# Silu from ScalarE's table two tiles at a time, and part of a state-space scan in PSUM, in a fused scan and expert kernel

## The chip, the cores and the metric

The kernel runs on one core of one Trainium2 chip. A core has TensorE (matrix products into PSUM), VectorE, ScalarE, GpSimd (POOL) and SyncE (SP, which issues transfers), each with its own instruction stream, tied by semaphores. The metric is device time in microseconds, the median of three runs. Lower is better.

## The reference

The input x is 2 x 2048 x 256, in fp32. After a layer norm two blocks run on it, and both are added to x.

```python
# block 1: tokens sorted by cluster, then for 256 channels and 16 states
dA = exp(d_t[..., None] * A)
h = dA * h + (d_t * u_t)[..., None] * b_t[:, None, :]
y = einsum('bdn,bn->bd', h, c_t)          # + D * u, and back to the old order
# block 2: 8 experts, top 2 of each token
h = silu(xt @ w1[e]) * (xt @ w3[e]);  y = h @ w2[e]
```

## The kernel before

A preparation makes the layer norm, the clusters, the gates, the sorted rows and, per chunk of 512 tokens, delta, delta * u, B and C, which go to DRAM (`dd_d`, `bc_d`). Then comes the loop. It has 64 **units** u (8 chunks c of 512 tokens, G = 8 groups g of 32 channels), and beside unit u stands expert tile j = u (128 tokens of one expert); 71 tiles in all, so the last seven form a tail. A partition of a unit is one of 32 channels and one of four sets of states; NH = 4 states lie beside one another along the row.

In unit u:

- SP loads the rows of delta and delta * u (`load_dd`), `late<-dd_d`, two buffers. ScalarE copies delta * u into the PSUM tile `pd` (`put_du`, L631) once VectorE's second product of the unit before has read the old one, and makes exp(delta * A) for the unit to come in one of four buffers of `ring` (`exps`, L620).
- VectorE runs `silu(j)` (L1009, L1012), then twice `half_unit`: a product delta * u * B of two states, 1024 wide, into PSUM `pb` (L968), and two scans of 512 from `ring` and `pb` into `ring` (L977). `keep_states` (L984) takes the four last columns.
- GpSimd multiplies the states by C in place (`multiply`, L473), two products of 1024, and then issues the gather of tile rows (L453) and the scatter-add of a finished tile (L460). In groups 3 and 6 it scatters two finished row blocks of the chunk before (L467) between its products, which are then 512 and 1536 wide.
- TensorE folds the products over states (`fold_states`, L1151, two units later), turns y (L1159), and for the expert tile runs `up` (four products with w1 into `fa`, four with w3 into `fb`, L1218), turns h (L1204) and the next x (L1188), the skip term (L1224) and `down` (w2, L1229). PSUM `pt` is shared by the turned h and the turned x; `py` by the down product, the folded sum and the turned y.
- ScalarE also runs `tanh(j)` (L688) on `fa`, and copies the turned h (L694), y rows (L641), the folded sum (L648), turned x (L654) and the weighted tile (L702) out of PSUM.

Each engine's order is written out by hand, one loop pass per tile; TensorE's is up(j), turn h(j-1), turn y(j-3), fold(j-2), turn x(j+1), skip and down(j-1). SP has one queue: weights of w3 and w2 for experts 0, 1 and 2 are loaded in the preparation and for 3 to 7 (ten loads of 512 KB) at unit 2, between the rows of unit 2 and those of unit 3.

## Time and profile before

| | us |
|---|---|
| median of three runs | 797.51 (797.41 to 798.80) |
| the profiled execution | 798.66 |
| its span | 796.9 |
| VectorE busy in the span | 681.3 (85%) |
| TensorE busy (modelled ends) | 650.7 (82%) |
| GpSimd busy | 596.8 (75%) |
| ScalarE busy | 420.1 (53%) |

The span is the time from the first to the last instruction that the profiler saw; the execution has 1.8 us around it. The shares are means over preparation, loop and tail. In rows of a timeline the first number is the start in us, the second the duration in us; xN merges N instructions; a bracket at the end gives the engine's idle time just before and what ended it. PE is TensorE, DVE VectorE, ACT ScalarE, POOL GpSimd. PEclk is the granted clock of TensorE as a share of 2.4 GHz.

### The profile page before, as it was taken

Reading aid. Unit: us, or ns where it says so; the run is one execution under the profiler, and the core shown is the slowest. Engines: PE = TensorE matmul, PEld = TensorE weight load, DVE = VectorE, ACT = ScalarE, POOL = GpSimd, SP = SyncE. Lnnn points to the kernel's source line nnn. Section 1 sums busy time; section 2 is a strip of 40 time slices with the busy share of each in tenths; the row PEclk is TensorE's granted clock in tenths of the full one; section 3 lists DMA queues with packets and bytes.
Section 4 is the critical chain, followed back from the end, with each engine's and each line's share of the span. In section 5 each row is a group of like instructions: output and inputs, shape, how many; then the busy total and the mean of one; then the engine's idle time right before and its main releaser. Section 6 shows DMA issues by size and latency. Waiting matters only on the chain.

```text
span 796.9 us, 13845 instructions
## 1 busy us (share of the span) xinstructions
PE 650.7 (82%) x4602; PEld 424.9 (53%) x4602; DVE 681.3 (85%) x883; ACT 420.1 (53%) x910; POOL 596.8 (75%) x371
## 2 busy tenths in 40 slices
PE   2633977777988898887989898899879898988992
PEld 1413855344655555655656555566556565555662
DVE  5858858897999999999899999989998999999120
ACT  1323657836666555655555655556555566554220
POOL 3727820166878889998989998888989899989642
PEclk9965989898999999999999999989989999999997
DMA  7982689996556744764475457537644754342331
GB/s 211 370 292 86 193 259 381 319 323 172 108 106 131 160 90 97 163 141 94 107 160 123 102 132 151 114 79 164 131 93 107 168 117 101 80 93 41 47 44 23
DMA packets 66275, 116.97 MB, mean 147 GB/s; under 512 B 12104, under 2 KB 46496, under 8 KB 64160
## 3 DMA queue, kind: packets, MB, share of 16 engines
q1 hardware_dynamic: 44048, 88.78, 38.5%
q0 software_dynamic: 19824, 27.16, 19.8%
q8 instruction: 40, 0.66, 0.3%
q10 hardware_dynamic: 2336, 0.15, 0.2%
q14 instruction: 27, 0.22, 0.1%
HBM read 80.78 MB, written 35.27 MB: 146 GB/s over the span
## 4 chain that ended last, share of the span: by engine, by line
DVE 38%; POOL 23%; PE 12%; issue 11%; DMA 11%; SPq 3%; ACT 2%; DVEq 0%; POOLq 0%; ACTq 0%
DVE ring L977 20%; POOL ring L473 11%; DVE pb L968 10%; POOL out_dram L460 4%; POOL out_dram L467 4%; DMA out_dram<-pool,tab 3%; PE py L1229 3%; DMA dd_d<-pool 3%; DVE pool L1009 2%; POOL pool L453 2%; DMA ring<-in_L_attn_x_dram 2%; PE fa L1218 2%; PE fb L1218 2%; PE py L1166 1%; POOL w2x L436 1%
## 5 line engine op out<-in xcount | busy, mean ns | idle before, releaser
L473 POOL TENSOR_TENSOR ring<-ring,bc 128x1024 f32<-128x1024 f32 (+1 forms) x127 | 305.9, 2426 | 34.2 <-DVE state L984 31.7
L977 DVE TENSOR_TENSOR_SCAN ring<-ring,state,pb 128x512 f32<-128x512 f32 x256 | 313.8, 1267 | 4.5
L620 ACT ACTIVATE ring<-late,aneg 128x512 f32<-128x512 f32 x256 | 164.6, 728 | 10.9 <-DMA late<-dd_d 10.9
L968 DVE TENSOR_TENSOR pb<-fb,bc 128x1024 f32<-128x1024 f32 x128 | 157.3, 1229 | 2.2
L1229 PE MATMUL py<-w2x,pool 128*128 x568 | 141.0, 393 | 0.0
L460 POOL DMA_INDIRECT out_dram<-pool,tab x71 | 113.7, 1602 | 34.0 <-DMA out_dram<-pool,tab 14.4
L1218 PE MATMUL fa<-w,pool 128*128 x284 | 136.3, 603 | 2.2 <-ACT pool L654 2.2
L1218 PE MATMUL fb<-w,pool 128*128 x284 | 133.5, 592 | 0.0
L453 POOL DMA_INDIRECT pool<-xn_d,tab x71 | 71.3, 1004 | 66.3 <-DVE ids L932 31.4
L1229 PEld LDWEIGHTS py<-w2x,pool 128*128 128x128 f32 x568 | 107.4, 200 | 12.9
L1151 PE MATMUL py<-ring,fold 128*32 128x128 f32 x2048 | 71.7, 282 | 26.9 <-POOL ring L473 26.9
L1218 PEld LDWEIGHTS fb<-w,pool 128*128 128x128 f32 x284 | 53.6, 191 | 65.8 <-issue 65.8
L688 ACT ACTIVATE pool<-fa 128x512 f32<-128x512 f32 x71 | 42.3, 596 | 83.2 <-PE fa L1218 83.2
L1224 PE MATMUL py<-skip,pool 128*128 128x128 f32 x284 | 51.1, 305 | 35.4 <-ACT y L648 29.9
L1009 DVE SCALAR_TENSOR_TENSOR pool<-pool,fa 128x512 f32<-128x512 f32 x71 | 48.2, 678 | 37.2 <-ACT pool L688 37.1
L1218 PEld LDWEIGHTS fa<-w,pool 128*128 128x128 f32 x284 | 54.8, 194 | 41.6 <-issue 37.9
L1151 PEld LDWEIGHTS py<-ring,fold 128*32 128x32 f32 x2048 | 53.7, 112 | 39.3 <-POOL ring L473 30.5
L1224 PEld LDWEIGHTS py<-skip,pool 128*128 128x128 f32 x284 | 39.6, 202 | 50.0 <-ACT late L641 42.8
L694 ACT COPY pool<-pt 128x512 f32<-128x512 f32 x71 | 41.5, 584 | 45.9 <-PE pt L1204 45.8
L467 POOL DMA_INDIRECT out_dram<-late,ids x32 | 50.5, 1578 | 15.5 <-issue 8.7
L641 ACT COPY late<-py 128x128 f32<-128x128 f32 x64 | 17.0, 265 | 83.4 <-PE py L1151 82.2
L1012 DVE SCALAR_TENSOR_TENSOR pool<-pool,fb 128x512 f32<-128x512 f32 x71 | 48.7, 686 | 9.0 <-PE fb L1218 6.9
(214 smaller groups left out, 732.8 us busy)
## 6 DMA issues: line engine op xcount, KB each, us to landing
late<-dd_d SPq DMA_DIRECT2D x256, 128.0 KB
bc<-bc_d SPq DMA_DIRECT2D x64, 256.0 KB
w<-in_L_ffn_w_dram SPq DMA_DIRECT2D x16, 512.0 KB, 7.7
ring<-in_L_attn_x_dram SPq DMA_DIRECT2D x8, 512.0 KB, 4.3
out_dram<-ring SPq DMA_DIRECT2D x8, 512.0 KB, 6.7
xn_d<-w2x SPq DMA_DIRECT2D x8, 512.0 KB, 8.0
dd_d<-pool SPq DMA_DIRECT2D x8, 512.0 KB, 7.1
w2x<-in_L_ffn_w_dram SPq DMA_DIRECT2D x8, 512.0 KB
```

The costliest lines, as they stand in the source:

```text
L453: po.indirect_dma_start(xr[j % XR], None, xn_d[:, :], bass.IndirectOffsetOnAxis(ap=tab.bitcast(U32)[:, j, 0:1], axis=0)).then_inc(xr_in[j ...
L460: po.indirect_dma_start(out[:, :], bass.IndirectOffsetOnAxis(ap=tab.bitcast(U32)[:, j, 0:1], axis=0), ye[j % YE], None, compute_op=ALU.add ...
L467: po.indirect_dma_start(out[:, :], bass.IndirectOffsetOnAxis(ap=ids[:, TPC * c + n:TPC * c + n + 1], axis=0), ya[c % 2][:, n, :], None, co ...
L473: return po.tensor_tensor(r, r, bc[:, u // G % 2, 1, states, :].rearrange("p n c -> p (n c)"), ALU.mult)
L620: ins = ac.activation(ring[:, u % RING, n, :], dd[:, u % 2, 0, :], ACT.Exp, scale=aneg[:, NH * g + n:NH * g + n + 1])
L968: ve.tensor_tensor(pb[:, :].rearrange("p (n c) -> p n c", n=2), pd[:, :].rearrange("p (o c) -> p o c", o=1).to_broadcast([P, 2, CH]), bc[: ...
L977: ve.tensor_tensor_scan(r, r, pb[:, CH * m:CH * m + CH], state[:, NH * g + n:NH * g + n + 1], ALU.mult, ALU.add).then_inc(S["scan_done"], 1)
L1009: ve.scalar_tensor_tensor(t, t, 1.0, fa[j % 2][:, :], ALU.add, ALU.mult).then_inc(S["s1_done"], 1)
L1151: ins = pe.matmul(pz[DG * q:DG * q + DG, 256:384], fold[:, :], ring[:, u % RING, n, P * q:P * q + P], start=(n == 0), stop=(n == NH - 1), ...
L1218: ins = pe.matmul(dst[:, :], xt[j % XT][:, P * k:P * k + P], w[:, bass.ds(e * (KC * H) + H * k, H)], start=(k == 0), stop=(k == KC - 1))
L1224: pe.matmul(py[:, P * k:P * k + P], xt[j % XT][:, P * k:P * k + P], skip[:, P * k:P * k + P], start=(k == 0), stop=False)
L1229: ins = pe.matmul(py[:, 0:D], ht[:, P * k:P * k + P], w2[:, bass.ds(e * (HC * D) + D * k, D)], start=False, stop=(k == HC - 1))
```

## The change

- `tanh(j)` becomes `gate(j)`, which takes silu from ScalarE's table "silu_and_others"; the exps need "exp_and_others". From tile 3 on ScalarE computes the gates of tiles j and j + 1 together in the passes of odd j, so the tables are changed twice in two tiles. TensorE therefore runs the w1 products of both tiles in the odd pass, on both sides of turn h, and turned x is made two tiles ahead.
- VectorE's silu is one product of the gate and `fb`. `silu(0)` moves behind unit 0.
- In groups 3, 4, 6 and 7 (not in unit 63) the fourth state is scanned into `pb`; VectorE multiplies it by C into `ring`, and copies its last column apart. GpSimd multiplies three states there.
- SP: expert 2's weights move from the preparation to unit 2; three experts are loaded before unit 3's rows and three behind them. SP itself waits until an expert's two loads have landed and counts that in `w_landed`, on which TensorE waits; behind unit 3's rows it waits for experts 2 to 7 before it goes on to the rows of unit 4.

```diff
 UNITS = NCH * G
-REST = UNITS + 1
+REST = UNITS + 2
+SINGLE = 3
+SHARED = (3, 4, 6, 7)
...
 HOT = 3
-EARLY = 3
+EARLY = 2
...
             eng.sem_inc(S["passed"], 1)
...
+        def shared(u):
...
+            return u % G in SHARED and u != UNITS - 1
...
+        def shares_by(u):
...
+            return sum(shared(v) for v in range(u + 1))
...
                 sp.dma_start(w2[:, e * HC * D:(e + 1) * HC * D].rearrange("p (k d) -> p k d", k=HC),
-                             w2_in[e].rearrange("(k p) d -> p k d", p=P)).then_inc(S["w2_in"], 16)
+                             w2_in[e].rearrange("(k p) d -> p k d", p=P)).then_inc(S[f"w_in{e}"], 16)
...
+            def count_landed(e):
...
+                sp.wait_ge(S[f"w_in{e}"], 32)
+                sp.sem_inc(S["w_landed"], 1)
...
                     load_down(0)
-                if c in (3, 4):
-                    if c == 3:
-                        sp.wait_ge(S["tab_ready"], 1)
-                    load_up(c - 2, w3, w3_in)
-                    load_down(c - 2)
+                if c == 3:
+                    sp.wait_ge(S["tab_ready"], 1)
+                    count_landed(0)
+                    load_up(1, w3, w3_in)
+                    load_down(1)
...
                     load_dd(1)
+                    count_landed(1)
...
                     load_dd(u)
-                if u == 2:
+                for e in {2: range(EARLY, 5), 3: range(5, E)}.get(u, ()):
+                    load_up(e, w3, w3_in)
+                    load_down(e)
+                if u == 3:
                     for e in range(EARLY, E):
-                        load_up(e, w3, w3_in)
-                        load_down(e)
+                        count_landed(e)
...
                         sp.wait_ge(S["hc_done"], G * c)
+                        sp.wait_ge(S["hd_done"], len(SHARED) * c)
...
                 if u < UNITS - 1:
-                    done = multiply(u, slice(split, NH))
+                    done = multiply(u, slice(split, NH - 1 if shared(u) else NH))
...
-            def tanh(j):
+            def gate(j):
                 ac.wait_ge(S["a_done"], j + 1)
-                ac.activation(sg[:, j % 2, :], fa[j % 2][:, :], ACT.Tanh, scale=0.5).then_inc(S["tanh_done"], 1)
+                if j >= 2:
+                    ac.wait_ge(S["htr_done"], j - 1)
+                ac.activation(sg[:, j % 2, :], fa[j % 2][:, :], ACT.Silu).then_inc(S["gate_done"], 1)
...
             exps(0)
-            tanh(0)
+            ac.preload_act_table_set("silu_and_others")
+            gate(0)
             evac_xt(1)
+            ac.preload_act_table_set("exp_and_others")
...
                 u = j
-                tanh(j)
+                first = j < SINGLE or j % 2
+                if first:
+                    ac.preload_act_table_set("silu_and_others")
+                    if j > 1:
+                        gate(j)
...
                     put_du(u)
+                if j == 1:
+                    gate(j)
                 evac_ht(j - 1)
+                if first:
+                    if j >= SINGLE:
+                        gate(j + 1)
+                    if u + 1 < UNITS:
+                        ac.preload_act_table_set("exp_and_others")
...
                     take_sum(u - 2)
-                if j + 1 < FT:
-                    evac_xt(j + 1)
+                ahead = j + 1 if j < SINGLE else j + 2
+                if ahead < FT:
+                    evac_xt(ahead)
...
                 evac_y(j - 1)
+                if j == SINGLE - 1:
+                    evac_xt(j + 2)
...
                     ve.wait_ge(S["scan_done"], 4 * u + 2 * half2)
+                if u and half2 == 0 and shared(u - 1):
+                    ve.wait_ge(S["hd_done"], shares_by(u - 1))
+                    ve.wait_ge(S["low_kept"], shares_by(u - 1))
...
                     n = 2 * half2 + m
-                    r = ring[:, u % RING, n, :]
-                    ve.tensor_tensor_scan(r, r, pb[:, CH * m:CH * m + CH], state[:, NH * g + n:NH * g + n + 1],
+                    r, b = ring[:, u % RING, n, :], pb[:, CH * m:CH * m + CH]
+                    ve.tensor_tensor_scan(b if n == NH - 1 and shared(u) else r, r, b, state[:, NH * g + n:NH * g + n + 1],
...
                 ve.wait_ge(S["scan_done"], 4 * u + 4)
-                ve.tensor_reduce(state[:, NH * g:NH * g + NH], ring[:, u % RING, :, CH - 1:CH], AX, ALU.max).then_inc(S["h_ready"], 1)
+                if not shared(u):
+                    ve.tensor_reduce(state[:, NH * g:NH * g + NH], ring[:, u % RING, :, CH - 1:CH], AX, ALU.max).then_inc(S["h_ready"], 1)
+                    return
...
+                top = pb[:, CH:2 * CH]
+                ve.tensor_reduce(state[:, NH * g:NH * g + NH - 1], ring[:, u % RING, 0:NH - 1, CH - 1:CH], AX, ALU.max).then_inc(S["h_ready"], 1)
+                ve.tensor_tensor(ring[:, u % RING, NH - 1, :], top, bc[:, u // G % 2, 1, NH - 1, :], ALU.mult).then_inc(S["hd_done"], 1)
+                ve.tensor_copy(state[:, NH * g + NH - 1:NH * g + NH], top[:, CH - 1:CH]).then_inc(S["low_kept"], 1)
...
-                ve.wait_ge(S["tanh_done"], j + 1)
+                ve.wait_ge(S["gate_done"], j + 1)
+                ve.wait_ge(S["b_done"], j + 1)
                 t = sg[:, j % 2, :]
-                ve.scalar_tensor_tensor(t, t, 1.0, fa[j % 2][:, :], ALU.add, ALU.mult).then_inc(S["s1_done"], 1)
-                ve.wait_ge(S["s1_done"], j + 1)
-                ve.wait_ge(S["b_done"], j + 1)
-                ve.scalar_tensor_tensor(t, t, 0.5, fb[0][:, :], ALU.mult, ALU.mult).then_inc(S["silu_done"], 1)
+                ve.tensor_tensor(t, t, fb[0][:, :], ALU.mult).then_inc(S["silu_done"], 1)
...
                 half_unit(u, 0)
+                half_unit(u, 1)
+                keep_states(u)
...
                     silu(u)
-                half_unit(u, 1)
-                keep_states(u)
...
                     ve.wait_ge(S["h_ready"], u + 1)
+                    ve.wait_ge(S["low_kept"], shares_by(u))
...
                     pe.wait_ge(S["hc_last"], 1)
+                if shared(u):
+                    pe.wait_ge(S["hd_done"], shares_by(u))
...
-            def expert_landed(name, j, e):
+            def expert_landed(j, e):
                 if j <= G:
-                    pe.wait_ge(S[name], e * 16 + 16)
+                    pe.wait_ge(S["w_landed"], e + 1)
...
                 pe.wait_ge(S["silu_done"], j + 1)
+                ahead = j + 2 if j + 1 < SINGLE else j + 3
+                pe.wait_ge(S["xt_done"], min(ahead, FT))
...
-            def up(j, e):
+            def up(j, e, w, dst, done):
+                for k in range(KC):
+                    ins = pe.matmul(dst[:, :], xt[j % XT][:, P * k:P * k + P],
+                                    w[:, bass.ds(e * (KC * H) + H * k, H)], start=(k == 0), stop=(k == KC - 1))
+                ins.then_inc(done, 1)
...
+            def up_gate(j, e):
                 pe.wait_ge(S["xt_done"], j + 1)
-                for w, dst, done in ((w1, fa[j % 2], S["a_done"]), (w3, fb[0], S["b_done"])):
-                    if w is w3:
-                        expert_landed("w3_in", j, e)
-                        if j:
-                            pe.wait_ge(S["silu_done"], j)
-                        if j >= REST:
-                            turn_h(j - 1)
-                    for k in range(KC):
-                        ins = pe.matmul(dst[:, :], xt[j % XT][:, P * k:P * k + P],
-                                        w[:, bass.ds(e * (KC * H) + H * k, H)], start=(k == 0), stop=(k == KC - 1))
-                    ins.then_inc(done, 1)
+                if j >= 2:
+                    pe.wait_ge(S["gate_done"], j - 1)
+                up(j, e, w1, fa[j % 2], S["a_done"])
...
+            def up_value(j, e):
...
+                expert_landed(j, e)
+                if j:
+                    pe.wait_ge(S["silu_done"], j)
+                up(j, e, w3, fb[0], S["b_done"])
...
                               stop=False)
-                expert_landed("w2_in", j, e)
...
             pe.wait_ge(S["pr_ut"], KC * (NCH - 1))
-            up(0, e_down)
+            up_gate(0, e_down)
...
             turn_x(1)
+            up_value(0, e_down)
...
                 u = j
+                e_next = expert_of(j + 1) if j + 1 < FT else None
                 if j == G + 1:
-                    pe.wait_ge(S["w3_in"], 16 * E)
-                    pe.wait_ge(S["w2_in"], 16 * E)
-                up(j, e_up)
-                e_next = expert_of(j + 1) if j + 1 < FT else None
-                if j < REST:
+                    pe.wait_ge(S["w_landed"], E)
+                if j < SINGLE:
+                    up_gate(j, e_up)
+                    up_value(j, e_up)
+                    turn_h(j - 1)
+                elif j % 2:
+                    up_gate(j, e_up)
+                    turn_h(j - 1)
+                    up_gate(j + 1, e_next)
+                    up_value(j, e_up)
+                else:
+                    up_value(j, e_up)
...
                 pe.wait_ge(S["ht_done"], j)
-                if j + 1 < FT:
-                    turn_x(j + 1)
+                ahead = j + 1 if j < SINGLE else j + 2
+                if ahead < FT:
+                    turn_x(ahead)
...
                 down(j - 1, e_down)
+                if j == SINGLE - 1:
+                    pe.wait_ge(S["xt_done"], j + 2)
+                    turn_x(j + 2)
```

VectorE, from the end of one unit to the next unit's first product. Before:

```order
L977 SCALAR_TENSOR_TENSOR ring<-ring,state,pb 128x512
L984 TENSOR_REDUCE state<-ring 128x4 [waits scan_done]
L1009 SCALAR_TENSOR_TENSOR pool<-pool,fa 128x512 [waits tanh_done]
L1012 SCALAR_TENSOR_TENSOR pool<-pool,fb 128x512 [waits b_done,s1_done]
L968 TENSOR_TENSOR pb<-fb,bc 128x1024 [waits scan_done,du_put]
```

After, behind a shared unit (group 4):

```order
L1017 SCALAR_TENSOR_TENSOR pb<-ring,state,pb 128x512
L1029 TENSOR_REDUCE state<-ring 128x3 [waits scan_done]
L1030 TENSOR_TENSOR ring<-pb,bc 128x512
L1031 COPY state<-pb 128x1
L1057 TENSOR_TENSOR pool<-pool,fb 128x512 [waits b_done,gate_done]
L1008 TENSOR_TENSOR pb<-fb,bc 128x1024 [waits hd_done,low_kept,scan_done,du_put]
```

One of the two silu steps is gone, and two instructions and one scan's target are new; the next unit's first product has two more waits.

TensorE, from the w1 products of an odd tile on (`fa1`), repeated rows left out. Before:

```order
L1218 ISA [waits xt_done]
L1218 MATMUL fa1<-w1,pool 128x512
...
L1218 REGISTER_ALU [waits silu_done]
L1218 MATMUL fb0<-w3,pool 128x512
...
L1204 MATMUL pt<-ident,pool 128x128 [waits silu_done]
...
L1159 MATMUL py<-ident,y1 128x128 [waits ya_done,y1_done,ye_done]
L1151 MATMUL py<-ring,fold 32x128 [waits y1_done,hc_done]
...
L1188 MATMUL pt<-ident,pool 128x128 [waits xr_in0,ht_done]
...
L1224 MATMUL py<-skip,pool 128x128 [waits y1_done,ya_done]
```

After, an odd tile and the start of the even one:

```order
L1259 ISA [waits gate_done,xt_done]
L1259 MATMUL fa1<-w1,pool 128x512
...
L1254 MATMUL pt<-ident,pool 128x128 [waits xt_done,silu_done]
...
L1259 ISA [waits gate_done,xt_done]
L1259 MATMUL fa0<-w1,pool 128x512
...
L1259 REGISTER_ALU [waits silu_done]
L1259 MATMUL fb0<-w3,pool 128x512
...
L1207 MATMUL py<-ident,y1 128x128 [waits ya_done,y1_done,ye_done]
L1199 MATMUL py<-ring,fold 32x128 [waits y1_done,hc_done]
...
L1236 MATMUL pt<-ident,pool 128x128 [waits xr_in1,ht_done]
...
L1259 REGISTER_ALU [waits silu_done]
L1259 MATMUL fb0<-w3,pool 128x512
```

The even tile's w1 products (`fa0`) moved ahead of the odd tile's w3 products (`fb0`).

ScalarE, from the weighted tile (L702, now L723) through the copies of one tile. Before:

```order
L702 ACTIVATE pool<-py,tab 128x256 [waits added,w2_done]
L688 ACTIVATE pool<-fa1 128x512 [waits a_done]
L631 COPY fb1<-late 128x512 [waits dbu_done]
L694 COPY pool<-pt 128x512 [waits htr_done]
L641 COPY late<-py 128x4x32 [waits sum_done,ytr_done]
L648 COPY y1<-py 128x128 [waits ytr_done,sum_done]
```

After, an odd tile:

```order
L723 ACTIVATE pool<-py,tab 128x256 [waits added,w2_done]
L737 ACT_TABLE_LOAD
L709 ACTIVATE pool<-fa1 128x512 [waits htr_done,a_done]
L650 COPY fb1<-late 128x512 [waits dbu_done]
L715 COPY pool<-pt 128x512 [waits htr_done]
L709 ACTIVATE pool<-fa0 128x512 [waits htr_done,a_done]
L749 ACT_TABLE_LOAD
L660 COPY late<-py 128x4x32 [waits added,sum_done,ytr_done]
L667 COPY y1<-py 128x128 [waits ytr_done,sum_done]
L673 COPY pool<-pt 128x256 [waits xtr_done]
```

Two table loads and a second gate stand in the odd pass; both gates are there, and the even pass has none.

## Rows read from the trace of the kernel before

**Rows 1.** Busy time; columns: stretch, us, PE, PEld, DVE, ACT, POOL, granted clock
```profile
200.00:735.00 535.00, 474.30 (x3502) 306.60 (x3504) 517.71 (x536) 308.25 (x647) 473.56 (x265) 0.97 0.54 117
```

**Rows 2.** Timeline of VectorE, one unit: start, duration (us)
```profile
507.25 0.16 DVE L984 TENSOR_REDUCE state<-ring 128x4 f32<-128x4 f32 x1
507.32 0.68 DVE L1009 SCALAR_TENSOR_TENSOR pool<-pool,fa 128x512 f32<-128x512 f32 x1
508.04 0.69 DVE L1012 SCALAR_TENSOR_TENSOR pool<-pool,fb 128x512 f32<-128x512 f32 x1
508.64 1.23 DVE L968 TENSOR_TENSOR pb<-fb,bc 128x1024 f32<-128x1024 f32 x1
...
516.14 0.16 DVE L984 TENSOR_REDUCE state<-ring 128x4 f32<-128x4 f32 x1
```

**Rows 3.** Timeline of VectorE, ends of units 0, 4 and 63
```profile
161.93 0.16 DVE L984 TENSOR_REDUCE state<-ring 128x4 f32<-128x4 f32 x1
...
202.42 0.16 DVE L984 TENSOR_REDUCE state<-ring 128x4 f32<-128x4 f32 x1
...
734.50 0.16 DVE L984 TENSOR_REDUCE state<-ring 128x4 f32<-128x4 f32 x1
```

**Rows 4.** Timeline of GpSimd and TensorE, a unit with scatter-adds, and an earlier fold
```profile
417.78 1.08 PE L1151 MATMUL py<-ring,fold 128*32 128x128 f32 x32 [1.71 <-POOL ring L473]
...
507.81 1.28 POOL L473 TENSOR_TENSOR ring<-ring,bc 128x512 f32<-128x512 f32 x1
...
513.26 4.02 POOL L473 TENSOR_TENSOR ring<-ring,bc 128x1536 f32<-128x1536 f32 x1
...
517.34 1.08 PE L1151 MATMUL py<-ring,fold 128*32 128x128 f32 x32 [3.00 <-POOL ring L473]
```

**Rows 5.** Busy time and granted clock (column after POOL) in two stretches
```profile
420.00:422.00 2.00, 2.00 (x7) 1.82 (x8) 1.96 (x3) 2.00 (x5) 1.98 (x2) 0.52 0.94 188
520.00:522.00 2.00, 2.00 (x8) 1.73 (x8) 1.97 (x3) 2.00 (x4) 1.97 (x2) 0.50 0.60 120
```

**Rows 6.** Timeline, TensorE's tile while it chases VectorE
```profile
526.72 1.88 PE L1218 MATMUL fb<-w,pool 128*128 x4
...
528.71 0.69 DVE L1012 SCALAR_TENSOR_TENSOR pool<-pool,fb 128x512 f32<-128x512 f32 x1 [0.47 <-PE fb L1218]
...
537.18 1.08 PE L1151 MATMUL py<-ring,fold 128*32 128x128 f32 x32
...
538.96 0.68 PE L1224 MATMUL py<-skip,pool 128*128 128x128 f32 x4 [0.33 <-ACT y L648]
...
541.21 1.88 PE L1218 MATMUL fa<-w,pool 128*128 x4
...
545.28 0.97 PE L1151 MATMUL py<-ring,fold 128*32 128x128 f32 x28
```

**Rows 7.** Timeline, TensorE's tile while it is ahead of VectorE
```profile
235.51 0.59 ACT L631 COPY fb<-late 128x512 f32<-128x512 f32 x1 [1.56 <-DVE pb L968]
...
238.08 0.68 PE L1224 MATMUL py<-skip,pool 128*128 128x128 f32 x4 [0.98 <-ACT y L648]
```

**Rows 8.** The page's costliest groups; count, busy us, mean ns, idle before
```profile
L977 DVE TENSOR_TENSOR_SCAN ring<-ring,state,pb 128x512 f32<-128x512 f32 x256 | 313.8, 1267 | 4.5
...
L968 DVE TENSOR_TENSOR pb<-fb,bc 128x1024 f32<-128x1024 f32 x128 | 157.3, 1229 | 2.2
```

**Rows 9.** Timeline of ScalarE, the one table load near the loop
```profile
154.06 1.28 ACT L688 ACT_TABLE_LOAD   x1
155.35 0.60 ACT L688 ACTIVATE pool<-fa 128x512 f32<-128x512 f32 x1
```

**Rows 10.** The chain that ended last: first weight load, unit 3's rows
```profile
156.34 0.43 SPq L283
...
171.20 10.04 DMA late<-dd_d
```

**Rows 11.** Waits between 100 and 165 us; in total, times, longest
```profile
DVE pool L943 <- DMA dd_d<-pool: 2.8, 2, 2.1
```

8 lines of the change are left out of this document (4 added, 4 removed).

## The prediction, made before the changed kernel ran

> **What bounds the kernel now.** I read the busy time by stage first. Up to some 154 us the tokens are prepared; from there 64 scan units run, until 735 us; then comes a tail of expert tiles. The stretch that matters is the loop [rows 1]. In the 535 us from 200 to 735 VectorE is busy 517.7 us (97%), GpSimd 473.6, TensorE 474.3 (modelled), ScalarE only 308.3. So the length of a VectorE unit sets the loop. One unit row by row [rows 2]: from reduce to reduce 516.14 - 507.25 = 8.89 us. In starts: reduce 0.07, the silu's first step 0.72, its second 0.60, then twice a product and its two scans, 7.50 in all (508.64 to 516.14).
>
> Next, where VectorE waits. Units 0 and 4 end at 161.93 and 202.42 [rows 3]: 40.49 for four, 4.9 more than 4 x 8.89, all of it at unit 3, which waits for its rows. Unit 63 ends at 734.50, which is 532.1 us for 59 units; 59 x 8.89 is 524.7, so 7.4 us are lost in the loop. They lie nearly all at units 25, 41 and 49. For unit 41 [rows 4, 5]: unit 38 ends at 507.25, GpSimd puts two scatter-adds between its products, whose last starts at 513.26 and ends at 517.28; TensorE has waited 3.00 us at the fold; then it runs at half clock for some 6 us (granted 0.50, 1.2 GHz), and VectorE is released late, at 528.71.
>
> How far off is TensorE as a bound? In a stretch where it chases [rows 6] its tile takes 537.18 to 545.28 = 8.10 us: fold to skip 1.78, skip and down 2.25 (538.96 to 541.21), w1 and w3 products 1.72 each, turning h and y 0.64 (4.07 from 541.21 to 545.28). Where it is ahead, it is tied to VectorE through ScalarE [rows 7]: the copy of du to PSUM starts as soon as the unit's second product has read the old one, at 235.51, 2.5 before the unit's end, and the skip starts 2.57 later.
>
> **The change part by part.**
>
> VectorE, silu. L1009 (71 times) goes, L1012 becomes a plain product of the same 128x512. Removed: 0.72 a unit. The new form has no row. The two nearest agree: the old second step, of the same operands, takes 0.69 (0.60 in starts); the 1024-wide product takes 1229 ns [rows 8], 1.04 ns an element above a fixed 160 if the 512-wide step is put beside it. Ends: 0.05 less and 0.05 more. I take no difference: a plain unit is 8.17.
>
> VectorE, shared units (3, 4, 6, 7 of each eight; not the last): the product with C, 512 wide out of PSUM, is added: 0.60 in starts; the one-column copy 0.07, as the reduce (158 ns, nearly all covered by its successor). 0.67 a unit. A scan that writes PSUM has no row. The nearest is L968 [rows 8], which already writes PSUM and shows no price for it; so 0. The other end is a scan that takes twice its 1.27 us (rival (d)); a gain is not expected, since a scan of 512 takes 1267 ns where a product of 512 takes 686: its steps, not its operands, set the length.
>
> Units 5 to 63: minus 59 x 0.72 = 42.5, plus 30 shared predecessors x 0.67 = 20.1: **22.4 less**.
>
> GpSimd: in shared units 512 elements less. A product of 512 takes 1.28 [rows 4], one of 1024 half of a pair's 4.69: 1.1 us less. It is relieved by 4.3 per eight units where VectorE is by 8 x 0.72 - 4 x 0.67 = 3.1, so it comes no nearer to being the bound.
>
> ScalarE: two table loads per two tiles in the loop. A load is 1.28 us and the next ACTIVATE starts at once [rows 9]. Silu for tanh: 0.60 for 0.60. ScalarE goes from 308/535 = 58% to about 58% x 8.89/8.51 + 2.57/17.0 = 75%. What hides them: the silu load lies after the old tile's y, beside the w1 products (skip + 2.24, a_done at + 4.1; y, load end at + 4.2), 0.1 late at most and for a value needed at + 8.1. The exp load lies beside the w3 products and the fold: ScalarE is through at + 9.25, and the fold at + 8.05 can be evacuated 1.20 later, at + 9.25. That is exact cover, with nothing over.
>
> TensorE: the same products in other order. Odd tile: w1 of j, turn h, w1 of j+1, w3 of j. After an even tile's skip, w3 of the odd tile starts at 2.25 + 1.72 + 0.44 + 1.71 = 6.12 and is seen done 1.99 later (526.72 to 528.71 [rows 6]), 8.11 in all. Tied to VectorE (skip 2.57 behind the du copy, which stands 2.6 before the next silu), it is done 10.68 after the du copy; VectorE wants it at 2.60 + 8.17 = 10.77 in the tightest case (third of eight). Slack 0.09; now, with 2.57 + 2.25 + 3.44 = 8.3 for the w3 products, it is nearly 4. A pair of tiles takes 16.2 at best against VectorE's mean pair of 17.0: TensorE keeps up, barely. So stalls stay. Where unit 6's scatters delay the fold: now it starts 517.34 - 507.41 = 9.9 after the unit's end; less 1.1 of product and about 0.8, since the add before the scatters comes sooner, it is about 8; the odd tile behind it (9th) is done at 8.0 + 1.8 + 8.1 = 17.9, wanted at 2 x 8.84 + 0.07 = 17.75. A few tenths, unless the clock halves, 3.3 us each. TensorE's idle time before that fold I work out as about 1.6 us (now 3.0); before other folds 1.71 us also was followed by half clock [rows 4, 5], so I count two halvings of six. Stalls: 2 x 3.3 + 1.4 for the rest = **8.0, against 7.4: 0.6 more**.
>
> SP and start. Unit 3's rows now stand behind 10 weight loads of 512 KB, the first issued at 156.34, and come in at 181.24 [rows 10]; after, behind 6. Ten loads and the rows in 24.9 us are 2.3 a load; alone on the queue a load would take 1.4 (0.52 MB at the page's best slice, 381 GB/s). So they land 5.6 to 9 sooner, before 176. Against it: expert 2's 1 MB moves from the preparation into this burst, SP then waits for all weights before it issues unit 4's rows (now issued before 175), and ScalarE's du copy of unit 4 is queued behind those exps. Also unit 1's w3 products now wait for silu(0), which moved behind unit 0. In order: preparation 1.3 sooner (VectorE waits 2.8 there for stores that stand behind expert 2's weights [rows 11]; bounds 0 and 2.8); unit 0 1.2 shorter, since silu(0) leaves it; unit 1 starts 2.1 after VectorE is free; unit 2 plain; unit 3 waits 1.0 for gate(3) behind a table load; unit 4 waits 1.8 for its du copy. The ends become 159.4, 170.3, 178.5, 187.7, 198.3 in place of 202.42: **4.1 less**, bounds 1 and 7.
>
> The tail, 62.4 us from unit 63's end to the span's end, is one of TensorE's tiles and their landing; its products are the same. 0, give or take 1.
>
> **Sum** against the profiled execution: 798.66 - 22.4 + 0.6 - 4.1 = 772.8; the median of the runs is 1.15 lower: 771.6.
>
> **Rivals.**
>
> (a) TensorE late: its idle time before unit 6's folds is not shorter and the clock halves in all seven. 5 more x 3.3 = 16.5: 788. For it: 3 of 6 do now, and slack is gone. Against: the faster product.
>
> (b) A table load costs more than its row, by as much again. The silu load has 4 us of room, the exp load none: the pair is 16.2 + 1.28 = 17.48 against 17.02, 0.46 x 30 pairs = 13.8: 785.4. Against it: 155.35 follows 154.06 by 1.29. Of this the Trainium skill, "ScalarE: Activation LUTs", What ACT_TABLE_LOAD costs, says that a load of 1283 ns has a drain of about 1380 ns behind it, and its Table sets section advises against changing sets in turns; this trace agrees with the 1283 and shows no drain. By the page's drain the sum would be an estimated 788.
>
> (c) Rows not sooner: SP's wait for all weights brings unit 4's rows so late that the start gains nothing: 775.7.
>
> (d) **Slower**: a scan that reads and writes one PSUM tile runs at half pace, 2.54 for 1.27: 31 x 1.27 = 39.4: 811. It is slower than before from 0.84 us a scan on. Nothing in the trace scans into PSUM.
>
> (e) (b) with four of (a)'s five extra halvings: 785.4 + 13.2 = 798.6, no change.
>
> **How the numbers follow.** Forecast 0.67, (a) 0.09, (b) 0.07, (c) 0.07, (d) 0.07, (e) 0.03. Likeliest: 771.6. The low end is no halving and all of the preparation's gain: 771.6 - 6.6 - 1.5 = 763.5; the high end takes in (a), (b) and (c), 788.5; (d) and (e) are left out, 0.10, and some tails. A measurement of this kernel can tell about 0.2% from no change. Faster 0.90, same 0.03, slower 0.07.
>
> **What would show it.** VectorE's unit of 8.17 and 8.84 in the trace after, the new product about 0.69, the scan into PSUM 1.27; unit 4's end near 198; table loads 1.28 each, 60-odd; VectorE's waits in the loop near 8 us, at the ninth units and on the w3 products. Wrong if the scan or the product out of PSUM is longer, if TensorE's pair is above 17.0, or if waits for gate or du appear in each pair.

## The result, and the profile after

| | before | after |
|---|---|---|
| median of the runs | 797.46 us | 788.42 us (783.5 to 795.57) |
| ratio to before | 1 | 0.986, 95% interval 0.981 to 0.990 |
| profiled execution's span | 796.9 | 793.9 |
| end of unit 0 / 4 / 63 | 161.93 / 202.42 / 734.50 | 163.43 / 204.18 / 732.47 |
| from unit 63's end to the span's end | 62.4 | 61.4 |

Forecast was 771.6 with a range of 763.5 to 788.5. The changed kernel is 1.0 to 1.9% faster, not 3.2%. Its runs spread over 12 us, and the profiled one is its longest; two more profiles of the same kernel stand below and are used beside it. They belong to other measurements on other chips, with medians of 784.26 us (0.982, 0.978 to 0.987) and 786.78 us (0.976, 0.970 to 0.982). Medians here are over all runs of a kernel, but the ratios leave out its slow runs, those over 1.5% above its fastest: one of four above, and three of the six behind 786.78, whose median is 782.31 without them.

VectorE's units first, as in [rows 2]: the timeline of one shared unit (start, duration, us), from the previous unit's end to this one's.

```profile
509.19 0.16 DVE L1029 TENSOR_REDUCE state<-ring 128x3 f32<-128x3 f32 x1
509.27 0.68 DVE L1030 TENSOR_TENSOR ring<-pb,bc 128x512 f32<-128x512 f32 x1
509.87 0.15 DVE L1031 COPY state<-pb 128x1 f32<-128x1 f32 x1
509.93 0.68 DVE L1057 TENSOR_TENSOR pool<-pool,fb 128x512 f32<-128x512 f32 x1
510.53 1.22 DVE L1008 TENSOR_TENSOR pb<-fb,bc 128x1024 f32<-128x1024 f32 x1
...
515.54 1.28 DVE L1017 TENSOR_TENSOR_SCAN ring<-ring,state,pb 128x512 f32<-128x512 f32 x1
516.74 1.26 DVE L1017 TENSOR_TENSOR_SCAN pb<-ring,state,pb 128x512 f32<-128x512 f32 x1
518.03 0.16 DVE L1029 TENSOR_REDUCE state<-ring 128x3 f32<-128x3 f32 x1
```

From reduce to reduce 8.84 us, the forecast's number. The scan into PSUM takes 1.26, as the one into SBUF; the product out of PSUM 0.68 (0.60 in starts), the copy 0.06 in starts, the silu's one step 0.60. A unit behind an unshared one takes 8.18.

The unit ends that answer to [rows 3], and the loop's busy times that answer to [rows 1] (stretch, us, PE, PEld, DVE, ACT, POOL, granted clock):

```profile
163.43 0.16 DVE L1025 TENSOR_REDUCE state<-ring 128x4 f32<-128x4 f32 x1
...
204.18 0.16 DVE L1029 TENSOR_REDUCE state<-ring 128x3 f32<-128x3 f32 x1
...
217.10 0.16 DVE L1025 TENSOR_REDUCE state<-ring 128x4 f32<-128x4 f32 x1
...
732.47 0.16 DVE L1025 TENSOR_REDUCE state<-ring 128x4 f32<-128x4 f32 x1
```

```profile
200.00:735.00 535.00, 481.64 (x3546) 309.96 (x3545) 501.39 (x540) 385.26 (x714) 443.37 (x267) 0.97 0.55 119
```

VectorE is now idle for 34 of 535 us instead of 17. Units 5 to 63 would take 502.1 (59 x 8.17 + 30 x 0.67); they took 732.47 - 204.18 = 528.3, so 26.2 us are lost where I had counted 8.0: 19.2 at six units, 4.1 at unit 5, the rest in small pieces. Behind unit 5 nearly all of it is one wait, for the w3 products (VectorE's waits between 213 and 700 us: in total, times, longest):

```profile
DVE pool L1057 <- PE fb L1259: 20.5, 9, 3.8
```

The 19.2 stand at units 17, 25, 33, 41, 49 and 57, which the forecast calls the ninth units: always at the odd tile behind the fold of a unit 6. Around unit 41, as [rows 4], GpSimd, TensorE and VectorE:

```profile
511.44 1.60 POOL L486 DMA_INDIRECT out_dram<-late,ids  x1 [0.73 <-DMA out_dram<-pool,tab]
...
513.34 1.56 POOL L486 DMA_INDIRECT out_dram<-late,ids  x1 [0.30 <-issue]
...
514.33 2.94 POOL L492 TENSOR_TENSOR ring<-ring,bc 128x1024 f32<-128x1024 f32 x1
...
517.33 1.08 PE L1199 MATMUL py<-ring,fold 128*32 128x128 f32 x32 [2.46 <-POOL ring L492]
...
521.01 3.10 PE L1283 MATMUL py<-w2x,pool 128*128 x8
...
529.81 0.69 DVE L1057 TENSOR_TENSOR pool<-pool,fb 128x512 f32<-128x512 f32 x1 [2.78 <-PE fb L1259]
```

The unit before ended at 509.19. The fold starts 8.1 us later, where I had put it; but TensorE has idled for 2.46, not 1.6, and the down products behind it take 3.10 instead of the 1.89 of an undisturbed tile. The 7 us behind each of the six folds (the last three columns are the granted clock, the DMA share and GB/s):

```profile
302.00:309.00 7.00, 6.81 (x47) 5.32 (x48) 6.86 (x10) 3.28 (x8) 6.01 (x4) 0.54 0.43 95
375.20:382.20 7.00, 6.63 (x50) 4.99 (x51) 6.89 (x7) 4.37 (x9) 5.56 (x4) 0.76 0.38 78
447.20:454.20 7.00, 6.82 (x50) 4.89 (x51) 6.72 (x10) 4.66 (x9) 5.14 (x4) 0.76 0.43 96
517.30:524.30 7.00, 5.72 (x47) 4.62 (x48) 6.90 (x9) 3.30 (x8) 5.93 (x4) 0.76 0.42 105
588.60:595.60 7.00, 6.91 (x47) 5.43 (x48) 6.86 (x10) 3.26 (x8) 6.17 (x4) 0.53 0.44 96
660.90:667.90 7.00, 5.75 (x48) 4.57 (x49) 6.89 (x8) 3.44 (x8) 5.98 (x4) 0.76 0.40 80
```

TensorE drops to its lower level (0.5 is 1.2 GHz) behind all six, for part or all of the stretch. Before, it did so behind three of six. The same 7 us in the kernel before, in front of units 33 (no fall) and 41 (fall):

```profile
445.10:452.10 7.00, 6.07 (x52) 4.23 (x53) 6.86 (x7) 3.97 (x9) 6.37 (x4) 1.00 0.36 77
517.30:524.30 7.00, 6.04 (x47) 4.92 (x48) 6.90 (x7) 3.25 (x7) 6.52 (x4) 0.63 0.29 52
```

The start: SyncE, ScalarE and VectorE around unit 4's rows.

```profile
176.20 0.47 SPq L350 DMA_DIRECT2D w2x<-in_L_ffn_w_dram  x1
...
178.86 2.56 ACT L639 ACTIVATE ring<-late,aneg 128x512 f32<-128x512 f32 x4 [0.75 <-DMA late<-dd_d]
...
186.35 0.69 DVE L1057 TENSOR_TENSOR pool<-pool,fb 128x512 f32<-128x512 f32 x1 [2.42 <-PE fb L1259]
...
188.22 1.72 SPq L339 DMA_DIRECT2D late<-dd_d  x4
...
193.23 2.56 ACT L639 ACTIVATE ring<-late,aneg 128x512 f32<-128x512 f32 x4 [5.04 <-DMA late<-dd_d]
```

Unit 3's rows do come sooner: their exponentials start at 178.86, not 181.27 [rows 10], and SyncE issues the last of the weights at 176.20. But then it waits for them, unit 4's rows are issued at 188.22, and its exponentials wait 5.04 us. VectorE waits 2.42 at unit 3, and unit 5 ends at 217.10, 12.9 behind unit 4. Whether SyncE's wait is what brings these rows late is tried below.

The difference from the forecast's span (772.8 less the 1.76 around it, 771.0) adds up: unit 4 ends 5.9 late, the loop loses 18.2 more, the tail is 1.0 shorter, 23.1 in all; 793.9 - 771.0 = 22.9.

### The profile page after: what moved, and what is told of

The parts are those of the page before. It is cut to its first block, busy times and chain, and to the rows that moved or that the text cites. A ratio compares the mean times of both kernels' runs of the same rounds, so it can differ in the third digit from the quotient of the medians.

```text
span 793.9 us, 14137 instructions
## 1 busy us (share of the span) xinstructions
PE 660.6 (83%) x4602; PEld 428.7 (54%) x4602; DVE 654.3 (82%) x874; ACT 506.9 (64%) x979; POOL 562.8 (71%) x371
## 4 chain that ended last, share of the span: by engine, by line
DVE 32%; POOL 21%; PE 17%; DMA 13%; issue 11%; SPq 3%; ACT 2%; DVEq 0%; ACTq 0%; POOLq 0%
DVE ring L1017 16%; DVE pb L1008 9%; POOL ring L492 7%; DMA out_dram<-pool,tab 6%; POOL xs_d L448 5%; POOL out_dram L486 4%; PE fa L1259 4%; PE py L1283 3%; DMA out_dram<-late,ids 2%; PE py L1199 2%; PE fb L1259 2%; POOL out_dram L479 2%; DVE pb L1017 2%; DMA w2x<-in_L_ffn_w_dram 1%; PE py L1279 1%
## 5 line engine op out<-in xcount | busy, mean ns | idle before, releaser
L492 POOL TENSOR_TENSOR ring<-ring,bc 128x1024 f32<-128x1024 f32 (+1 forms) x127 | 272.3, 2162 | 48.4 <-DVE state L1025 34.4
L1017 DVE TENSOR_TENSOR_SCAN ring<-ring,state,pb 128x512 f32<-128x512 f32 x225 | 277.5, 1269 | 4.6
L479 POOL DMA_INDIRECT out_dram<-pool,tab x71 | 112.7, 1587 | 43.7 <-DMA out_dram<-pool,tab 16.5
L1283 PE MATMUL py<-w2x,pool 128*128 x568 | 142.6, 397 | 0.0
L1259 PE MATMUL fb<-w,pool 128*128 x284 | 135.3, 599 | 3.1 <-DVE pool L1057 3.1
L1283 PEld LDWEIGHTS py<-w2x,pool 128*128 128x128 f32 x568 | 109.0, 202 | 13.3
L1057 DVE TENSOR_TENSOR pool<-pool,fb 128x512 f32<-128x512 f32 x71 | 48.5, 683 | 67.3 <-PE fb L1259 67.2
L1259 PEld LDWEIGHTS fb<-w,pool 128*128 128x128 f32 x284 | 54.3, 192 | 56.9 <-issue 55.2
L650 ACT COPY fb<-late 128x512 f32<-128x512 f32 x64 | 37.8, 590 | 59.8 <-DVE pb L1008 59.7
L1259 PEld LDWEIGHTS fa<-w,pool 128*128 128x128 f32 x284 | 51.6, 192 | 39.5 <-issue 37.7
L1279 PEld LDWEIGHTS py<-skip,pool 128*128 128x128 f32 x284 | 40.0, 203 | 49.3 <-ACT late L660 44.1
L1254 PEld LDWEIGHTS pt<-ident,pool 128*128 128x128 f32 x284 | 35.8, 142 | 37.8 <-issue 37.7
L448 POOL DMA_INDIRECT xs_d<-w2x,pos_a x32 | 38.3, 1196 | 23.6 <-DVE pos_a L885 14.1
## 6 DMA issues: line engine op xcount, KB each, us to landing
w2x<-in_L_ffn_w_dram SPq DMA_DIRECT2D x8, 512.0 KB, 10.7
```

The source lines that it names most:

```text
L448: po.indirect_dma_start(dst[:, :], bass.IndirectOffsetOnAxis(ap=index[:, t:t + 1], axis=0), row[:, t, 0:dst.shape[1]], None).then_inc(done ...
L479: po.indirect_dma_start(out[:, :], bass.IndirectOffsetOnAxis(ap=tab.bitcast(U32)[:, j, 0:1], axis=0), ye[j % YE], None, compute_op=ALU.add ...
L492: return po.tensor_tensor(r, r, bc[:, u // G % 2, 1, states, :].rearrange("p n c -> p (n c)"), ALU.mult)
L1017: ve.tensor_tensor_scan(b if n == NH - 1 and shared(u) else r, r, b, state[:, NH * g + n:NH * g + n + 1], ALU.mult, ALU.add).then_inc(S["s ...
L1259: ins = pe.matmul(dst[:, :], xt[j % XT][:, P * k:P * k + P], w[:, bass.ds(e * (KC * H) + H * k, H)], start=(k == 0), stop=(k == KC - 1))
L1279: pe.matmul(py[:, P * k:P * k + P], xt[j % XT][:, P * k:P * k + P], skip[:, P * k:P * k + P], start=(k == 0), stop=False)
```

## The experiments

All times below are medians of 6 or 12 runs of a kernel; the kernel before, beside them, had 797.96 to 800.20. A ratio is to it, with its 95% interval. The changed kernel ran beside the experiments on two of the five chips only; where it didn't, kernels are compared by their ratios.

**The changed kernel twice more.**

> The changed kernel once more, unchanged. Theory N (the number of half-clock episodes differs from run to run): the median stays at 786 to 790 and a second profile has VectorE's units at 8.18 and 8.84 again, but its stalls at the ninth units sum to another number than the 26 us of the first profile, by 3 us or more, and its start of the loop lies 1 to 3 us elsewhere. Theory F (all of the lost time is in the order of the work): the stalls are the same within 1 us.

> The changed kernel, unchanged, as the measure of the other kernels on this chip: by both theories 784 to 790, its stalls at the ninth units 14 to 23 us together, each behind a fold that starts 8.0 to 10.3 us after unit 6's end and at which TensorE had waited over 2.2 us.

Measured 784.26 (0.982, 0.978 to 0.987) and, on another chip, 786.78 us. Stalls at the ninth units: 19.2 us in the first profile, 15.4 and 19.2 in these. The fold behind unit 6 starts 9.1 us after the unit's end in the mean of the 18 cases (8.1 to 10.3), TensorE idle before it for 2.8 (1.8 to 4.0), and the clock falls behind all 18. Unit 4 ends at 200.49 and 201.71, and unit 5 takes 8.9 in both: the 4 us lost there in the first profile come and go. From unit 5 on the loop loses 26.2, 16.3 and 20.0 us in the three, so theory N holds and F falls, though the median of 784.26 is below N's 786. Of the first profile's shortfall some is luck of that run; the stalls at the ninth units are not.

These profiles also show the slack of each place, as the time from the modelled end of a tile's w3 products to the silu product that reads them, less the 0.11 us that is left where VectorE waits. In front of the third unit of eight it is 0.16 us (0.09 forecast), in front of the ninth, where no scatters delay the fold (unit 9), 1.65, and at even tiles from tile 4 on 2.0 to 4.4.

**Clock or lateness.** TensorE kept busy ahead of the late fold.

```diff
+WARM = 24
...
-                pe.transpose(pz[:, 384:512], y1[:, :], ident[:, :]).then_inc(S["ytr_done"], 1)
+                for _ in range(WARM if u % G == G - 3 and u > G else 1):
+                    ins = pe.transpose(pz[:, 384:512], y1[:, :], ident[:, :])
+                ins.then_inc(S["ytr_done"], 1)
```

> Ahead of each fold that waits for GpSimd's two scatters of unit 6, TensorE repeats the transposition of y 24 times instead of once, some 2.5 us of work in an idle stretch of 2.5. Theory B1 (the stalls at every ninth unit are the half clock behind that idle stretch, 3.3 us each): the granted clock stays at full behind these folds, each stall falls from about 3.4 to about 0.8 us, six times, so 14 to 16 us less, 772 to 774. Rival B2 (the stalls are the late fold alone, and the clock only goes with it): 788, no change, or longer by the added work, up to 3 us.

Measured 777.80 us (0.974, 0.971 to 0.978), 6.5 less than the changed kernel on the same chip. The granted clock behind the six folds, first and last:

```profile
295.50:302.50 7.00, 6.65 (x56) 4.61 (x57) 6.89 (x9) 5.75 (x11) 6.18 (x4) 1.00 0.41 87
...
644.70:651.70 7.00, 6.64 (x56) 4.59 (x57) 6.86 (x10) 5.76 (x11) 6.18 (x4) 1.00 0.45 96
```

It is 1.00 in all six, and the stalls at the ninth units fall from 15.4 to 6.7 us. B1 holds for the cause, not for the size: with the clock kept up, 0.3 to 1.7 us stay at each, which is the late fold itself, and two of the folds were now late behind the repeats. By the difference to the profiles above (15.4 and 19.2) the clock costs 1.5 to 2.1 us at each of the six; the lateness costs about 1.1.

The repeats are not the only evidence. In two kernels below, whose folds behind unit 6 are as in the changed kernel, the clock stayed up once each by itself. One is the changed kernel with silu(0) moved back. The fold in front of its unit 33, and the 7 us behind it:

```profile
446.70 1.08 PE L1199 MATMUL py<-ring,fold 128*32 128x128 f32 x32 [2.56 <-POOL ring L492]
446.70:453.70 7.00, 6.67 (x56) 4.62 (x57) 6.68 (x11) 5.58 (x11) 5.40 (x4) 1.00 0.45 101
```

TensorE idled for 2.56 us there and the stall is 0.5 us, while the five others of that profile, behind a fallen clock, are 3.4 to 4.6. The other is the second of those with tanh, in front of unit 25: 3.09 us idle, clock 1.00, a stall of 1.5 beside 1.7 to 3.0. In the six profiles of the changed kernel and of these two the clock falls behind 34 of 36 such folds.

**The scatters behind both products.**

```diff
-                split = 1 if scans else NH // 2
+                split = NH // 2
...
-                for n in scans:
-                    add_scan(c - 1, n, landed_scan(c - 1, scans[0]) - 16)
...
                 done.then_inc(S["hc_done"], 1)
+                for n in scans:
+                    add_scan(c - 1, n, landed_scan(c - 1, scans[0]) - 16)
```

> GpSimd issues the scatters of the scan rows of units 3 and 6 behind both of the unit's products and not between them. Theory B (the late fold, with or without the clock, makes the stalls): the fold after unit 6 starts some 3 to 5 us sooner, TensorE doesn't wait for it, the stalls at the ninth units go, 6 x 3 to 3.4 us, 768 to 772. Rival: GpSimd, busy 88% of the loop, is now late with the next unit's product by the 3.2 us of the scatters, the stall moves to the tenth unit, 784 to 790.

Measured 797.42 us (0.999, 0.996 to 1.002): slower than the changed kernel by 13. The stalls at the ninth units are gone, and 29.8 us stand elsewhere, most of it two units sooner (unit 23: 6.0). GpSimd's timeline tells why:

```profile
338.10 1.56 POOL L486 DMA_INDIRECT out_dram<-late,ids  x1 [0.30 <-issue]
345.22 1.55 POOL L479 DMA_INDIRECT out_dram<-pool,tab  x1 [5.56 <-DMA out_dram<-late,ids]
...
348.11 3.57 POOL L492 TENSOR_TENSOR ring<-ring,bc 128x1024 f32<-128x1024 f32 x2
```

Each scatter-add waits until the one before has landed. Put right behind one another, scan rows and expert rows make GpSimd wait 5.56 us for a landing; the product between them had covered most of that. The rival was right that GpSimd would be late, and too low with its 784 to 790; the stalls went two units back, not one on. Theory B's 768 to 772 fell.

**Scatters in unit 7.** The same scatters, moved to the unit whose fold is followed by an even tile.

```diff
-SCAN_UNITS = {3: (0, 1), 6: (2, 3)}
+SCAN_UNITS = {3: (0, 1), 7: (2, 3)}
```

> The second two scatters of the scan rows go from unit 6 of each eight to unit 7; nothing else is changed. The fold that they delay is then followed by an even tile, whose w3 products stand right behind the skip's and have about 4 us of slack, and no longer by an odd tile with 0.09. Theory B (the late fold costs only because the odd tile behind it has no slack): the stalls at the ninth units go, and none takes their place, 14 to 18 us less than the changed kernel beside it, 768 to 773, though TensorE still idles over 2 us at the fold and its clock still halves. Rival B3 (GpSimd, or the clock, is late with or without the slack): the stalls move to another unit of the eight, and less than 5 us is gained.

Measured 779.01 us (0.976, 0.972 to 0.979) beside 786.78 for the changed kernel on the same chip, 7.8 less by all runs. Beside the 782.31 of the runs that its ratio counts it is 3.3 less, and the two ratios are the same, 0.976: how much time the line saves is not measured well by these runs. The traces are clearer. VectorE's waits between 213 and 700 us, first of the changed kernel beside it, then of this one:

```profile
DVE pool L1057 <- PE fb L1259: 18.7, 6, 4.0
```

```profile
DVE pool L1057 <- PE fb L1259: 4.3, 7, 2.4
```

The stalls at the ninth units are gone (19.2 to 0.1 us), and none of their size took their place; 0.3 us each came up at the third units, 2.5 once at unit 35. From unit 5's end to unit 63's it takes 499.0 us, not 513.3. But the tail is longer: 64.3 to 65.2 us in the seven profiles with this line, 60.9 to 61.4 in the three of the changed kernel. At its end stands a chain of scatter-adds, each of which waits for the one before, and the last four scatters of scan rows in it begin 23.1 us behind unit 63's end, not 19.4. So of the 14.3 us some 4 are lost again in the tail. Theory B was right on where the stalls go, and wrong on 768 to 773.

One more expectation was wrong: TensorE does not idle 2 us before the folds of unit 7 (at most 0.4), and its clock doesn't fall behind them. In the next kernel, which has the same scatters:

```profile
509.75 1.59 POOL L486 DMA_INDIRECT out_dram<-late,ids  x1 [0.16 <-issue]
...
511.65 1.56 POOL L486 DMA_INDIRECT out_dram<-late,ids  x1 [0.30 <-issue]
...
512.67 2.94 POOL L492 TENSOR_TENSOR ring<-ring,bc 128x1024 f32<-128x1024 f32 x1
...
515.66 1.08 PE L1199 MATMUL py<-ring,fold 128*32 128x128 f32 x32
```

The scatters wait for no landing there and start 1.7 us after the unit's end (508.07), where unit 6's start 2.2 to 4.4 after it; the fold starts 7.6 behind the unit, without a wait. So this run shows that the place costs the time; it does not tell slack from the earlier start. The slack at the even tile behind this fold is 3.0 us with and without scatters in unit 7.

**The wait for the weights.** SyncE issues two more units' rows first.

```diff
-                if u == 3:
+                if u == 5:
                     for e in range(EARLY, E):
                         count_landed(e)
```

> SyncE issues unit 4's and unit 5's rows before it waits for the weights of experts 2 to 7. Theory A (the rows of unit 4 come late behind that wait, and make TensorE and with it units 4 and 5 late): the copy of du for unit 4 starts when the unit before has read the old one, unit 4 ends by about 200 and unit 5 by about 208, 5 to 7 us sooner than in the profile of the changed kernel, and the time falls by 4 to 7 us, to 782. Rival (the rows then stand behind the weights on the DMA engines all the same): less than 1.5 us.

> The same, and SyncE issues unit 4's and 5's rows before it waits for the weights of experts 2 to 7. Theory A (that wait brings the rows late): unit 5 starts 1 to 5 us sooner than in the kernel beside it, 1 to 4 us less in the median, 765 to 771. Rival (the rows stand behind the weights on the DMA engines anyway): the same median within 1 us.

Measured 781.40 (0.979, 0.975 to 0.982) beside 784.26 of the changed kernel, with overlapping intervals; and, on top of the scatters in unit 7, 772.89 (0.969, 0.965 to 0.972) beside 779.01, where the intervals don't touch. (The forecast for it was 765 to 771.) The traces say less than the medians: from unit 0's end to unit 5's, 49.3 us is the mean of five profiles with this edit (47.3 to 51.0, silu(0) and pairs as changed), 50.8 that of the nine without (48.5 to 54.3); the forecast had 47.7. The two ranges overlap, so I take no more than 1.5 us from the traces; the 6 of the second pair of medians are not explained by it.

Theory A's mechanism falls in these traces. Without the edit SyncE issues unit 4's rows 22.8 to 25.9 us behind unit 0's end and ScalarE's exponentials for unit 4 start at 27.0 to 31.9. With it the rows are issued at 13.2 to 15.2, some 10 us sooner, and the exponentials start at 27.7 to 29.4, no sooner, and still wait 2.0 to 4.1 us for the rows. The rows are late whether or not SyncE waits for the weights, as the rival had it. In the kernels further below that issue fewer weights ahead of unit 4's rows, these exponentials start at 23.0 to 24.6 without a wait, and unit 5's wait 2.6 and 4.8 us instead.

In the profile of the last kernel unit 5 onward loses next to nothing (VectorE's waits between 213 and 700 us, then the 7 us behind one of the folds, clock 1.00):

```profile
DVE pool L1057 <- PE fb L1259: 1.4, 5, 0.3
```

```profile
515.60:522.60 7.00, 6.13 (x56) 4.27 (x55) 6.86 (x9) 5.22 (x11) 6.16 (x5) 1.00 0.50 116
```

**Table loads.** Tanh for silu, no table loads in the loop.

```diff
-                    ac.preload_act_table_set("silu_and_others")
...
-                        ac.preload_act_table_set("exp_and_others")
...
-                ac.activation(sg[:, j % 2, :], fa[j % 2][:, :], ACT.Silu).then_inc(S["gate_done"], 1)
+                ac.activation(sg[:, j % 2, :], fa[j % 2][:, :], ACT.Tanh).then_inc(S["gate_done"], 1)
```

> The changed kernel with tanh in place of silu on ScalarE and no changes of the function table in the loop; the sigmoid's halving and the product with x are left out, so what is computed differs, the instructions but for the table loads are as many and as long. Theory T0 (the table loads are hidden, my term of 0): the same median within 2 us, 783 to 786. Rival T1 (the pair of loads of 1.28 us delays ScalarE's copies on which TensorE waits: the turned h, y, the sum): TensorE gets through an odd tile's w3 products 1 us and more sooner, the stalls fall, 6 us and more less, 778 or below.

> Tanh in place of silu and no changes of the function table in the loop (the sigmoid's halving and the product with x are left out), beside the changed kernel on the same chip. Theory T0 (table loads hidden): within 3 us of the changed kernel beside it, and the stalls at the ninth units as long. Rival T1 (each pair of loads holds TensorE up): 6 us and more less.

Measured 790.50 us (0.989, 0.984 to 0.994) on one chip and 782.49 (0.981, 0.978 to 0.985) on another, beside the changed kernel's 786.78 there (782.31 by the runs that its ratio counts). VectorE's waits between 213 and 700 us in the two profiles:

```profile
DVE pool L1051 <- PE fb L1253: 22.6, 7, 4.7
```

```profile
DVE pool L1051 <- PE fb L1253: 13.0, 6, 2.9
```

Without the loads the six stalls are still there, and VectorE's waits as large as with them (14.9 to 20.5 in the three profiles of the changed kernel). T1 falls: the loads don't make them. A load in the changed kernel, ahead of a gate:

```profile
309.47 1.28 ACT L737 ACT_TABLE_LOAD   x1
310.77 0.60 ACT L709 ACTIVATE pool<-fa 128x512 f32<-128x512 f32 x1
```

T0 holds within what is measured: the medians differ by 4.3 us over all runs and by 0.2 over those that the ratios count (0.976 and 0.981, intervals overlapping). A microsecond or two isn't told from nothing. On the other chip the changed kernel didn't run, and 790.50 is outside T0's 783 to 786.

**No shared units.**

```diff
-SHARED = (3, 4, 6, 7)
+SHARED = ()
```

> The changed kernel with no shared units: GpSimd multiplies all four states by C in each unit, VectorE scans them all into SBUF. Only the silu part, the order of TensorE and the start are left. VectorE would need 8.17 a unit, 20 us less in all; GpSimd's loop grows by 31 x 1.1 = 34 us, from 451 to some 485 busy, beside 482 of VectorE. Theory P (GpSimd is then the bound, its waits for the landing of its own scatters on top): 790 to 800, VectorE's waits 30 us and more. Rival (GpSimd just keeps up): 770 to 776.

Measured 805.90 us (1.010, 1.005 to 1.016), later even than P. The silu part alone, with the order of TensorE's tiles and the start that it brings, makes the kernel 1% slower than before. VectorE's waits between 213 and 700 us are

```profile
DVE pool L1057 <- PE fb L1259: 45.7, 19, 6.4
```

GpSimd then multiplies 512 elements more in half of the units. Its total, 471 of the 535 us busy between 200 and 735, is still no bound; 30.8 of the 51 us lost from unit 6 on stand at the ninth units. The folds behind unit 6 start 11.4 to 12.5 us after its end there, 9.1 in the changed kernel. That is a late fold in front of odd tiles again, so the shared units seem to pay by bringing folds forward, not by GpSimd's total; this reading has no run of its own.

**silu(0).** Back between the halves of unit 0, once on the changed kernel and once on the best one.

```diff
                 half_unit(u, 0)
+                if u == 0:
+                    silu(u)
                 half_unit(u, 1)
                 keep_states(u)
-                if u == 0:
-                    silu(u)
```

> silu(0) on VectorE stands between the two halves of unit 0, as in the kernel before, and not behind the unit. Theory C (behind unit 0 it makes TensorE late by some 3 us at tile 1, and this lateness shows as VectorE's waits at units 1 and 3): unit 0 becomes 0.7 longer, the waits at units 1 and 3, 2.7 to 4 and 2.6 us so far, fall together by 3 to 5 us, unit 5 starts 2 to 4 us sooner than the 201.3 of the changed kernel's second profile, 781 to 783. Rival (the order of tiles 2 to 4, where single tiles turn into pairs, makes unit 3's wait): unit 1's wait goes, unit 3's stays at 2.6 us or grows by what unit 1 gave, less than 1 us gained.

> On that kernel silu(0) of VectorE stands between the two halves of unit 0. Theory C: the waits at units 1 and 3, 5.5 us together, fall to below 3 us, unit 5 ends 2 to 3 us sooner, 768 to 770. Rival C3 (TensorE at the start is late by the preparation's projections and its own half clock, not by silu(0)): the wait at unit 1 gets shorter and that at unit 3 longer by as much, the same median within 1 us.

Measured 790.06 us (0.989, 0.986 to 0.993) for the first, not 781 to 783: unit 1 loses 1.3 us in its profile, not 3.4 to 4.0, and unit 3 loses 6.4, so the rival holds. For the second 782.03 us (0.979, 0.974 to 0.984), beside 779.61 without the edit. VectorE's waits between 150 and 205 us, without and with it:

```profile
DVE pool L1057 <- PE fb L1259: 4.1, 2, 2.2
```

```profile
DVE pool L1057 <- PE fb L1259: 2.7, 1, 2.7
DVE pool L1057 <- ACT pool L709: 0.7, 1, 0.7
```

Unit 1 now loses 0.8 us and not 2.9, unit 3 loses 2.8 and not 2.0, and unit 0 is longer by the 0.6 of the step. C falls: the two together stay above 3 us and the median isn't lower. C3 came nearer, since part of unit 1's wait turned up at unit 3; but not as much as unit 1 gave, and the median is 2.4 us higher, with overlapping intervals, where C3 had it within 1.

**When pairs begin, and the weights spread.** Both on the kernel with the scatters in unit 7 and the wait at unit 5.

```diff
-SINGLE = 3
+SINGLE = 5
```

```diff
-                for e in {2: range(EARLY, 5), 3: range(5, E)}.get(u, ()):
+                for e in {2: range(EARLY, 4), 3: range(4, 6), 4: range(6, E)}.get(u, ()):
```

> The kernel with unit 6's scatters in unit 7 and the rows of units 4 and 5 ahead of the weights' wait, unchanged, as the measure of the other kernels on this chip: 772 to 774, VectorE's wait at unit 3 of 2.4 to 2.8 us in its profile.

> On that kernel, tiles 3 and 4 are done singly, pairs begin at tile 5. Theory C1 (unit 3's wait is the first pair, which TensorE, some 3 us behind since unit 1, reaches without slack): unit 3's wait falls from 2.5 to below 0.5 us and none comes at unit 5, since TensorE has caught up by then; 2 to 3 us less, 770 to 771. Rival C2 (TensorE doesn't catch up with singles, the wait moves to unit 5): the same median within 1 us.

> On that kernel, SyncE issues the weights of experts 2 and 3 behind unit 2's rows, of 4 and 5 behind unit 3's, of 6 and 7 behind unit 4's (2 to 4 behind unit 2's and 5 to 7 behind unit 3's so far). Theory A2 (rows behind weights on the DMA engines still cost time at units 3 to 5): 1 to 2 us less. Rival (with the wait moved, the rows are early enough; VectorE's waits at units 1 and 3 are on TensorE alone): the same median within 0.7 us.

> The version with unit 6's scatters in unit 7, the weights spread over units 2 to 4 and the wait for them at unit 5, once more, as the measure: 770 to 774, 0.967 to 0.975 of the kernel before; VectorE's waits on TensorE 3 to 4 us at unit 1, 2 at unit 3, next to none from unit 5 on.

The measure had 774.93 us (0.974, 0.970 to 0.979), singles to tile 4 777.15 (0.975, 0.972 to 0.979), the spread weights 771.91 (0.971, 0.967 to 0.976) and, once more on another chip, 779.61 (0.975, 0.971 to 0.978). With singles the wait at unit 3 falls to 0.4 us, and units 2, 4 and 5 lose 1.5, 1.6 and 2.3: C2. The spread takes 0.5 us from unit 3's wait; the medians don't tell it from nothing. The same kernel differs by 7.7 us between two chips, 771.91 and 779.61 (forecast for the repeat: 770 to 774), and by 0.004 in its ratio to the kernel before beside it: times of different chips can't be compared, ratios can, within their intervals.

**Three edits at once**: the wait at unit 5, silu(0) between the halves, and the repeats, with 10 more ahead of the fold of unit 5.

> Three edits of the changed kernel together: SyncE issues unit 4's and 5's rows before it waits for the weights; silu(0) between the halves of unit 0; TensorE repeats the transposition of y 24 times ahead of the fold that waits for unit 6's scatters, and 10 times ahead of the fold of unit 5. If the three causes add up: 777.8 (the repeats alone) less 2 to 3 for the weights' wait, less 3 for silu(0), less 1 to 2 for the clock behind the fold of unit 5: 770 to 773. If they are one cause counted twice (all of them only make TensorE less late): 775 to 778.

Measured 785.30 us (0.983, 0.979 to 0.987), no better than the changed kernel and above both forecasts. The clock is 1.00 on average between 213 and 700 us, but the folds now start 9.2 to 12.8 us behind unit 6 with no wait before them: the repeats themselves make TensorE late, and the stalls at the ninth units are 14.1 us with the clock up. Filler work is only free up to the idle time, which differs from turn to turn.

**The kernel before with its scatters in unit 7.** The edit is the one line above.

> The kernel before with unit 6's two scatters in unit 7, nothing else changed. Theory B (late fold behind the scatters, in this kernel with 4 us of slack behind it and so only 3 stalls of six): its stalls at units 25, 41 and 49, some 7 us, go, 790 to 792. Rival (single tiles are all alike here, so the stall moves to the tenth unit): the same median within 2 us.

Measured 797.90 us (1.000, 0.998 to 1.002). The three stalls go (7.1 us in all at units 25, 41 and 49); 3.0 in four smaller ones come at units 34, 42, 50 and 58, and the tail is 2.2 longer, 796.9 - 732.29 = 64.6. So B's stalls went as it said, and the rival was right on the median and on the tenth unit. Three of the four folds of unit 7 behind which the clock falls there, with TensorE idle for 2.9 to 3.1 us, cost 0.4 to 0.5 us; the fourth, 4.3 us idle, costs 1.6. VectorE's waits between 213 and 700 us:

```profile
DVE pool L1012 <- PE fb L1218: 1.8, 4, 0.5
DVE pool L1009 <- ACT pool L688: 1.1, 1, 1.1
```

Single tiles are alike, so the slack is the same at both places (3.6 us in front of units 9 and 10, where nothing is late), and what the move gave here is the earlier fold: 8.6 to 8.7 us behind its unit in five of six turns, not 9.3 to 10.7. The same one-line move is worth nothing before the change; after it, it takes 14.3 us from the loop and gives some 4 back in the tail.

## Why the prediction was wrong, point by point

- **VectorE's units: right.** 8.18 and 8.84 measured, 8.17 and 8.84 forecast; the 22.4 us less are there. Rival (d) is out: 1.26 us for a scan into PSUM.
- **Table loads: right as a term of 0, as far as measured.** 1.28 us each, the next ACTIVATE at once, and the stalls are there without them. So rival (b), with its 13.8 us, is out, and with it the drain of which the Trainium skill, "ScalarE: Activation LUTs", speaks under What ACT_TABLE_LOAD costs; no row here shows it.
- **TensorE's stalls: the step that failed.** The slack of 0.09 us was worked out rightly (0.16 measured), and so was the price of lateness: 0.15 for a fold at 8.0, hence 0.85 for one at 8.7 and 1.15 for one at 9.0, where 0.85 and 1.12 were left with the clock kept up. But I put the fold at 8.0 behind unit 6 in each of the six turns; it comes at 9.1 in the mean, since GpSimd waits before the scatters in most turns, for up to 1.9 us, mostly for a landing. And I put TensorE's idle time at 1.6, from which I counted two halvings of six; it is 2.8, and the clock falls behind 18 folds of 18. The term of 8.0 us measured 15.4 to 19.2 at the ninth units alone and 16.3 to 26.2 in all. That is the mechanism of rival (a), to which I gave 0.09; it was the likelier one on the forecast's own numbers: before, 3.00 idle and half clock, and no row said that the shorter product would shorten that. That the first median, 788.42, falls on (a)'s 788 is luck: (a) had 16.5 us more at the folds and the start as forecast, the runs 7 to 11 more at the folds and the rest elsewhere.
- **The price of a halving: too high by itself.** 3.3 us, which the prediction gives without a sum; 1.5 to 2.1 measured. The rest of each stall is lateness, which I had at a few tenths.
- **The start: failed in three places.** Counted 4.1 sooner; unit 4 ends 0.7 and 1.9 sooner in two profiles, 1.8 later in the third, and unit 5 up to 5.8 later. From unit 0's end to unit 1's it takes 11.1 to 12.9 us where silu(0) stands behind unit 0, not 10.9. Unit 3 loses 2.0 to 2.8 us, waiting for the w3 products, in 14 of the 17 profiles with pairs from tile 3 (3.3 to 6.6 in the others), where I had 1.0 for the gate. It seems that TensorE, behind since unit 1, meets the first pair without slack; each edit only moved this wait. And unit 4's rows come late, so that ScalarE waits 2.5 to 5.0 us for them in the three profiles; the effect is that of rival (c), but not its reason, since they came no sooner when SyncE issued them 10 us earlier.
- **The preparation: not contradicted, and not shown.** Unit 0 ends at 160.2 in the mean of 15 profiles with this preparation, 159.4 forecast; but from 157.6 to 166.4, and at 161.93 and 163.32 in the only two of the kernel before. In such a spread the agreement is partly luck.
- **The tail: 1.0 to 1.5 shorter** in three profiles, about the 0 plus or minus 1.

The change gave 22.4 us on VectorE and took 8 to 12 back at the ninth units, beyond the 7.1 of before. Two edits here give much of it back: TensorE kept busy ahead of the fold (0.974 of the kernel before) and the scatters in unit 7 (0.976). Scatters in unit 7 with the wait for the weights behind unit 5's rows ran at 0.969 and 0.974 on two chips, and with the weights spread as well at 0.971 and 0.975; these can't be told apart, and they are near the 0.967 that the forecast had for the change alone. That is no support for the forecast, which had these stalls at 8.0 without such edits. Open stay the waits at units 1 and 3, some 5 us, which only moved in each experiment; how much of the good of unit 7 is slack and how much the earlier fold; and the last microseconds of the table loads.

## What to carry to other kernels

TensorE, which here gets its work in pairs of tiles, had 2.0 to 4.4 us of slack in front of one half of the pair, and in front of the other, where nothing was late, from 2.3 down to 0.2. Work out the slack for each place of the period, and put what comes late in front of the place that has it, before anything is made faster. Where an engine waits for another's scatter-adds, count the landing of the one before them in every turn, not in the one turn that was read. A fall of the clock behind an idle stretch costs only what the slack behind it doesn't absorb: 0.4 to 0.5 us in the kernel before with its scatters in unit 7, 1.5 to 2.1 us in the changed kernel. And when a stall is gone from the loop, look at the tail before counting the gain.

## What the runs showed of the hardware

A scan that reads its second operand from a PSUM tile and writes its result over it takes 1.26 us for 512 elements, no more than one into SBUF.

TensorE's clock in the preparation differs from run to run of the same kernel, and the start of the loop with it. Between 120 and 150 us (us, PE, PEld, DVE, ACT, POOL, clock) in the profile with the latest start and in one of the earliest:

```profile
120.00:150.00 30.00, 29.40 (x142) 19.18 (x144) 18.09 (x33) 16.49 (x31) 1.96 (x2) 0.63 0.71 252
```

```profile
120.00:150.00 30.00, 26.12 (x157) 16.57 (x158) 24.61 (x42) 23.74 (x46) 2.72 (x2) 0.84 0.94 336
```

At 0.63 unit 0 ends at 166.35, at 0.84 at 158.29. The two kernels differ only behind this stretch. What makes the clock fall there wasn't tried. So a difference of a few microseconds between the spans of two single profiles of this kernel says nothing of an edit.
